# Attention stage: products with reciprocals on another engine, extra work at other steps, fewer and larger transfers, two banks for the last output products

## The reference

```python
q = einsum('bsd,de->bse', layernorm(x), Wq)      # 16 heads of 32
k = einsum('bsd,de->bse', ctx, Wk); v = einsum('bsd,de->bse', ctx, Wv)
qh, kh = rope(split(q)), rope(split(k)); vh = split(v)
attn = softmax(einsum('bhqd,bhkd->bhqk', qh, kh) / sqrt(32))
x = x + einsum('bsd,de->bse', merge(einsum('bhqk,bhkd->bhqd', attn, vh)), Wo)
x = x + ffn(layernorm(x), w_gate, w_up, w_down)  # act_qdq: one scale per whole tensor
```

## Time and profile before

| | us |
|---|---|
| median of 3 runs | 2434.16 (2432.11 to 2439.43) |
| the profiled execution | 2446.6 |
| its span, first to last instruction | 2444.7 |
| PE busy in the span | 2251.5 (92%) |
| DVE / ACT / POOL busy | 1712.5 / 1284.4 / 607.5 |
| attention stage | 0 to 892.5 |

### The profile page before, as it was taken

How to read it: one execution, slowest core, us unless ns; L and a number is a source line. 1 busy time by engine, 2 the same in 40 slices (tenths; PEclk the granted TensorE clock), 3 DMA queues, 4 the chain that set the end, 5 groups by cost and what they waited for, 6 DMA issues and landing times.

```text
span 2444.7 us, 32311 instructions
## 1 busy us (share of the span) xinstructions
PE 2251.5 (92%) x12763; PEld 1002.3 (41%) x12763; DVE 1712.5 (70%) x1750; ACT 1284.4 (53%) x1184; POOL 607.5 (25%) x432
## 2 busy tenths in 40 slices
PE   4698999999998759999999899999999499999999
PEld 2353343333433224444444344444444144444444
DVE  5466788887886646645553179888888797777772
ACT  3235454454543303322332288888887587777771
POOL 2463444444443201100110045444444000000000
PEclk9899999999999979999999999999999799999999
DMA  7443656465555656788876498777778365555551
GB/s 184 108 131 92 169 161 178 142 184 150 163 148 160 152 151 201 243 266 249 269 246 214 176 332 309 291 288 287 289 287 309 147 234 217 216 217 215 217 218 60
DMA packets 307913, 505.57 MB, mean 207 GB/s; under 512 B 208172, under 2 KB 210476, under 8 KB 270892
## 3 DMA queue, kind: packets, MB, share of 16 engines
q1 hardware_dynamic: 307756, 503.45, 62.8%
HBM read 248.83 MB, written 186.65 MB: 178 GB/s over the span
## 4 chain that ended last, share of the span: by engine, by line
PE 78%; DVE 7%; issue 6%; DMA 3%; POOL 3%; ACT 2%; SPq 2%; DVEq 0%; POOLq 0%; ACTq 0%
PE banks L1250 41%; PE banks L1647 19%; PE banks L535 5%; PE banks L577 4%; PE banks L516 2%; PE banks L554 2%; PE banks L594 1%; DVE MX L983 1%; PE banks L599 1%; PE banks L498 1%; DVE A L956 1%; POOL AH L1117 1%; PE banks L495 1%; POOL QW L1076 1%; DMA AH<-in_ctx 1%
## 5 line engine op out<-in xcount | busy, mean ns | idle before, releaser
L1647 PE MATMUL banks<-W,OH 128*128 128x512 f16 x2304 | 501.1, 381 | 37.1 <-DVE OH L1726 37.1
L1250 PE MATMUL banks<-XB,W 128*128 128x512 f16 x2304 | 500.3, 381 | 22.9 <-DMA XB<-XC 22.9
L1250 PE MATMUL banks<-XB,WT 128*128 128x512 f16 x2304 | 500.4, 381 | 8.2 <-DMA XB<-xt_s 8.2
L1270 ACT ACTIVATE OB<-banks,uns 128x512 f32<-128x512 f32 x384 | 254.3, 683 | 425.9 <-PE banks L1250 419.4
L1647 PEld LDWEIGHTS banks<-W,OH 128*128 128x128 f16 x2304 | 226.1, 98 | 312.1 <-issue 39.5
L1250 PEld LDWEIGHTS banks<-XB,W 128*128 128x128 f16 x2304 | 226.1, 98 | 297.1 <-DMA XB<-XC 23.4
L1250 PEld LDWEIGHTS banks<-XB,WT 128*128 128x128 f16 x2304 | 226.1, 98 | 282.5 <-DMA XB<-xt_s 8.7
L1515 POOL TENSOR_TENSOR PR<-GS,OB 128x2048 f32<-128x2048 f32 x47 | 225.4, 4795 | 274.3 <-ACT OB L1270 254.7
L1339 DVE TENSOR_REDUCE amx<-OB 128x1 f32<-128x2048 f32 x48 | 109.7, 2285 | 241.5 <-ACT OB L1270 241.5
L577 PE MATMUL banks<-XC,AH 128*128 128x512 f16 x768 | 182.9, 389 | 16.8 <-DVE RX L943 16.7
L535 PE MATMUL banks<-XD,WQ 128*128 128x512 f16 x768 | 187.2, 396 | 0.0
(11 more groups left out here) (213 smaller groups left out, 2832.8 us busy)
## 6 DMA issues: line engine op xcount, KB each, us to landing
g_s<-OB SPq DMA_DIRECT2D x48, 1024.0 KB, 5.7
GL<-g_s SPq DMA_DIRECT2D x48, 1024.0 KB, 8.2
up_s<-OB SPq DMA_DIRECT2D x48, 1024.0 KB, 4.9
XA<-up_s SPq DMA_DIRECT2D x32, 1024.0 KB, 9.3
gq_s<-GQ SPq DMA_DIRECT2D x48, 512.0 KB, 5.2
XD<-gq_s SPq DMA_DIRECT2D x48, 512.0 KB, 6.7
XA<-in_x SPq DMA_DIRECT2D x16, 1024.0 KB, 7.2
QW<-QE SPq DMA_DIRECT2D x128, 128.0 KB, 2.8
```

Of the source, the lines that this page charges most:

```text
L1250: t = e.matmul(pk[:].rearrange("p (j t) -> p j t", j=4), WT[w][:, ot, wa, kk, :], XB[i % 2][:, xa, :, kk, :], start=(kk == 0 and wa == 0 a ...
L1270: e.activation(OB[n % 3][:, r, :], bank[k % 8][:], ACT.Copy, scale=uns[:, 12 * w + ot:12 * w + ot + 1]).then_inc(s_ev, 1)
L1647: t = e.matmul(pk[:].rearrange("p (r n) -> p r n", r=4), OH[i % 2][:, a, ot, j * 128:(j + 1) * 128], WD[:, :, c, wa, o4, :], start=(ot == ...
```

## The change

- The products of A with the reciprocals (L956) go from DVE to POOL, for all units but the last four. POOL's order in a step becomes: cosine product, products of normal_at(s), sine product, residuals of normal_at(s).
- A unit's reciprocals come by one transfer instead of four.
- In SP's stream X1 is stored before the next x is loaded.
- Weight rows are handled two steps later (w_step(k) = 17 + 4k), so DVE scales in c == 2 steps. A batch's aggregate L970 and the deviation that POOL makes of it go from the c == 3 step to the following c == 0 step, on DVE behind L983 (st2 has two halves).
- The output products of the last eight units run two in a step, in banks 4 and 5 by turns, so there are four steps fewer.
- The last batch's four units are normalised in one step, by DVE, from four buffers of their own (QR); their sums and reciprocals are sent from ACT's queue instead of SP's.
- The weight transposes begin at step 60 instead of 62.

```diff
-NSTEP = NU + 16
+NSTEP = NU + 12
+LATE = NU - 8
...
 def normal_at(s):
     b, c = divmod(s - 13, 4)
-    return [4 * b + 2 * c, 4 * b + 2 * c + 1] if 0 <= b < B and c < 2 else []
+    if s == NSTEP - 4:
+        return list(range(NU - 4, NU))
+    return [4 * b + 2 * c, 4 * b + 2 * c + 1] if 0 <= b < B - 1 and c < 2 else []
+def output_at(s):
+    u = s - 15
+    if u < LATE:
+        return [u] if u >= 0 else []
+    u = LATE + 2 * (u - LATE)
+    return [u, u + 1] if u < NU else []
+def deviations_at(s):
+    if s == NSTEP - 1:
+        return [B - 1]
+    return [output_at(s - 2)[-1] // 4] if output_at(s - 2) and (output_at(s - 2)[-1] + 1) % 4 == 0 and s > 15 else []
 def w_step(k):
-    return 15 + 4 * k
+    return 17 + 4 * k
 def build(nc, x, ctxt, wq, wk, wv, wo, w_gate, w_up, w_down, cosq, sinq, cosk, sink, eye, out, scr):
...
         s_rd = sem("s_rd")
-        s_rb = sems("s_rb", 2)
+        s_rb = sems("s_rb", 4)
...
         rs1 = sbufs(st, "rs1", 2, [128, 8])
-        st2 = sbuf(st, "st2", [128, 4, 6])
+        st2 = sbuf(st, "st2", [128, 2, 4, 6])
...
+        def rb(u):
+            if u < NU - 4:
+                return RB[u % 2][:], s_rb[u % 2], 16 * (u // 2 + 1)
+            i = u - NU + 4
+            return QR[i][:], s_rb[i], 16 * ((NU - 4) // 2 + 1) if i < 2 else 16
+        def o_bank(u):
+            return bank[4] if u >= LATE and u % 2 == 0 else bank[5]
...
-        def sp_recip(e, u):
+        def dma_recip(e, u):
...
             e.wait_ge(s_rd, 16 * (b + 1))
-            if u >= 2:
+            if u >= NU - 4:
+                e.wait_ge(s_c1, NU - 4)
+            elif u >= 2:
                 e.wait_ge(s_an, u - 1)
+            to, sem_, _ = rb(u)
+            e.dma_start(to, sr_d[1 + b % 2, 4 * c:4 * c + 4, :].unsqueeze(1).to_broadcast([4, 32, 512])).then_inc(sem_, 16)
+        def dma_sums_out(e, b):
+            e.wait_ge(s_rc, b + 1)
             for g in range(4):
-                e.dma_start(RB[u % 2][32 * g:32 * g + 32, :], sr_d[1 + b % 2, 4 * c + g:4 * c + g + 1, :].to_broadcast([32, 512])).then_inc(s_rb[u % 2], 16)
+                e.dma_start(sr_d[0, g:16:4, :], RC[32 * g:32 * g + 4, :]).then_inc(s_rg, 16)
+        def dma_sums_in(e, b):
+            e.wait_ge(s_rg, 64 * (b + 1))
+            e.dma_start(RG[:], sr_d[0].rearrange("r (e f) -> (r e) f", f=64)).then_inc(s_rl, 16)
+        def dma_recip_out(e, b):
+            e.wait_ge(s_rr, 2 * (b + 1))
+            e.dma_start(sr_d[1 + b % 2].rearrange("r (e f) -> (r e) f", f=64), RG[:]).then_inc(s_rd, 16)
         def sp_attention(e):
...
-                if c == 3 and 0 <= b - 2 < B:
-                    e.wait_ge(s_rc, b - 1)
-                    for g in range(4):
-                        e.dma_start(sr_d[0, g:16:4, :], RC[32 * g:32 * g + 4, :]).then_inc(s_rg, 16)
+                if c == 3 and 0 <= b - 2 < B - 1:
+                    dma_sums_out(e, b - 2)
                 for u in normal_at(s + 1):
-                    sp_recip(e, u)
-                u = s - 14
-                if 0 <= u < NU:
+                    if u < NU - 4:
+                        dma_recip(e, u)
+                for u in output_at(s - 1):
+                    e.wait_ge(s_x1, u + 1)
+                    e.dma_start(x1_d[u // 4, :, u % 4, :], X1[u % 2]).then_inc(s_x1d[u % 2], 16)
+                for u in output_at(s + 1):
...
                     e.dma_start(XR[u % 2], x1_rows(u // 4)[:, u % 4, :]).then_inc(s_xr[u % 2], 16)
-                u = s - 16
-                if 0 <= u < NU:
-                    e.wait_ge(s_x1, u + 1)
-                    e.dma_start(x1_d[u // 4, :, u % 4, :], X1[u % 2]).then_inc(s_x1d[u % 2], 16)
-                if c == 3 and 0 <= b - 2 < B:
-                    e.wait_ge(s_rg, 64 * (b - 1))
-                    e.dma_start(RG[:], sr_d[0].rearrange("r (e f) -> (r e) f", f=64)).then_inc(s_rl, 16)
+                if c == 3 and 0 <= b - 2 < B - 1:
+                    dma_sums_in(e, b - 2)
...
-                if c == 3 and 0 <= b - 2 < B:
-                    e.wait_ge(s_rr, 2 * (b - 1))
-                    e.dma_start(sr_d[1 + b % 2].rearrange("r (e f) -> (r e) f", f=64), RG[:]).then_inc(s_rd, 16)
+                if c == 3 and 0 <= b - 2 < B - 1:
+                    dma_recip_out(e, b - 2)
...
-                if 62 <= s < 62 + NO:
-                    t = s - 62
+                if 60 <= s < 60 + NO:
+                    t = s - 60
...
         def pe_output(e, u):
             b, j = divmod(u, 4)
-            if u:
+            if u == LATE:
+                e.wait_ge(s_mte, B)
+            elif u > LATE:
+                e.wait_ge(s_x1, u - 1)
+            elif u:
...
                 for wa, a in THREE:
-                    t = e.matmul(BO_, AH[b % 2][:, a, k, j * 128:(j + 1) * 128], WO[:, wa, k, :],
+                    t = e.matmul(o_bank(u), AH[b % 2][:, a, k, j * 128:(j + 1) * 128], WO[:, wa, k, :],
...
                     pe_kv(e, i)
-                if 0 <= s - 15 < NU:
-                    pe_output(e, s - 15)
+                for u in output_at(s):
+                    pe_output(e, u)
...
                     e.activation(RC[:], BS_, ACT.Copy).then_inc(s_rc, 1)
+                    if b - 2 == B - 1:
+                        dma_sums_out(e, B - 1)
+                        dma_sums_in(e, B - 1)
+                        dma_recip_out(e, B - 1)
+                        for u in range(NU - 4, NU):
+                            dma_recip(e, u)
         def dve_amax(e, n):
...
+        def dve_x1_aggregate(e, b):
+            e.wait_ge(s_st2, 12 * b + 10)
+            for i in range(4):
+                t = e.bn_aggr(mv2[:, 4 * b + i, :], st2[:, b % 2, i, :])
+            t.then_inc(s_mv2, 1)
         def dve_v_max(e, g):
...
-                u = s - 16
-                if 0 <= u < NU:
-                    ob, j = divmod(u, 4)
+                for u in output_at(s - 1):
...
                         e.wait_ge(s_st2, 3 * (u - 2) + 3)
-                    e.scalar_tensor_tensor(X1[u % 2], BO_, vun[:, 2:3], XR[u % 2], ALU.mult, ALU.add).then_inc(s_x1, 1)
+                    e.scalar_tensor_tensor(X1[u % 2], o_bank(u), vun[:, 2:3], XR[u % 2], ALU.mult, ALU.add).then_inc(s_x1, 1)
...
                 for u in normal_at(s):
-                    e.wait_ge(s_rb[u % 2], 64 * (u // 2 + 1))
-                    e.wait_ge(s_a, u + 1)
-                    e.tensor_tensor(A[:, u % 6, :], A[:, u % 6, :], RB[u % 2][:], ALU.mult).then_inc(s_an, 1)
-                u = s - 16
-                if 0 <= u < NU:
+                    if u >= NU - 4:
+                        to, sem_, n = rb(u)
+                        e.wait_ge(sem_, n)
+                        e.wait_ge(s_a, u + 1)
+                        e.tensor_tensor(A[:, u % 6, :], A[:, u % 6, :], to, ALU.mult).then_inc(s_an, 1)
+                for u in output_at(s - 1):
...
                     e.wait_ge(s_x1, u + 1)
-                    if j == 0 and ob:
-                        e.wait_ge(s_mv2, ob)
-                    e.bn_stats(st2[:, j, :], X1[u % 2]).then_inc(s_st2, 1)
+                    if j == 0 and ob >= 2:
+                        e.wait_ge(s_mv2, ob - 1)
+                    e.bn_stats(st2[:, ob % 2, j, :], X1[u % 2]).then_inc(s_st2, 1)
...
                     e.tensor_reduce(xmn[:, u:u + 1], X1[u % 2], AX.X, ALU.min).then_inc(s_st2, 1)
-                    if j == 3:
-                        e.wait_ge(s_st2, 3 * u + 1)
-                        for i in range(4):
-                            t = e.bn_aggr(mv2[:, 4 * ob + i, :], st2[:, i, :])
-                        t.then_inc(s_mv2, 1)
+                    if u >= NU - 1:
+                        dve_x1_aggregate(e, ob)
...
+                if s >= 16 and output_at(s - 2) and (output_at(s - 2)[-1] + 1) % 4 == 0 and output_at(s - 2)[-1] < NU - 1:
+                    dve_x1_aggregate(e, output_at(s - 2)[-1] // 4)
...
+                for u in normal_at(s):
+                    if u < NU - 4:
+                        to, sem_, n = rb(u)
+                        e.wait_ge(sem_, n)
+                        e.wait_ge(s_a, u + 1)
+                        e.tensor_tensor(A[:, u % 6, :], A[:, u % 6, :], to, ALU.mult).then_inc(s_an, 1)
+                if s < NU:
+                    pool_rope_sine(e, ROT["q", s])
...
                     e.tensor_tensor(AH[nb % 2][:, 1, nc_, :], A[:, u % 6, :], AH[nb % 2][:, 0, nc_, :], ALU.subtract).then_inc(s_alo, 1)
-                if s < NU:
-                    pool_rope_sine(e, ROT["q", s])
...
                     pool_deviation(e, b + 2)
-                u = s - 19
-                if c == 3 and 0 <= u < NU:
-                    ob = u // 4
+                for ob in deviations_at(s):
...
```

## The result

| | before | after |
|---|---|---|
| median (us) | 2433.14 (2427.72 to 2439.43) | **2560.64** (2558.43 to 2562.72) |
| profiled execution / its span | 2446.6 / 2444.7 | 2561.1 / 2559.3 |
| mean granted clock of TensorE | 0.968 | 0.947 |

The ratio of after to before is 1.0511, 95% interval 1.0495 to 1.0527: 5.1% slower, 127 us by the medians (115 by the two profiled spans, of which the one before was 0.5% over its median). The forecast was 2466 us, range 2438 to 2496. The sign and the new wait were as forecast, the size was not; the time lies 65 us above the range (2560.64 against 2496).

What follows compares the result with a forecast made beforehand. TensorE was taken as the bound, with 47.4 us to win in the attention stretch. +34.8 (stretch) + 5 (first batch) - 8 (tail) = +31.8 us, added to the median 2434.16, gave 2466 us, range 2438 to 2496.

Steps and rivals of the forecast that it cites:

- stretch: Attention from 278.65 to 775.14 us, 46 steps: 12 x (4.85 + 2.0) = 82.2 us in place of 47.4, +34.8 us.
- What bounds the kernel: Attention stretch: TensorE is the bound, 449.1 us without stalls against 496.5, so only 47.4 us can be won.
- The new wait: Each batch: ACT's A copy waits for the first residual, exponential P queues behind, PE stands 4.85 us before the largest-score product.
- landing of the exchange: SP's half exchange QW in the c == 1 step: lands 2.8 us after its second issue, at t = 13.5 from that step's scores.
- rival 3: Exchange leaves right behind QE, both new waits end in time, stall at most 1.4 us: -39 us, 2396 us; chance 0.08.
- rival 4: Products of 1.6 us and landings of 3.9 give a 6.8 us stall and 2.7 us of clock: 2502 us; chance 0.11.
- The issue at t = 11.2: SP, t counted from the c == 1 step's scores: the exchange's second issue was forecast at t = 10.7.
- The clock: TensorE falls to 1.2 GHz after the new wait in all 12 batches, 2.0 us each.
- The tail: Last batch's reciprocals and last eight units' output products: end at about 864.5 us, -8 us, bounds -5 and -12.
- The weights and SP's order: Weight scaling moved to c == 2 on DVE: 0, up to 1 us a batch; SP's store and load order was passed over.
- 1: The stall comes but TensorE's clock holds: +7 us, 2441 us; chance 0.10.
- 2: The copy's wait is covered; ACT's AH and MT, behind GpSimd's products, delay the scores 2.5 us: +1 us, 2435; chance 0.07.

Runs made afterwards that it cites:

- a_resid: Changed kernel with GpSimd's residuals put ahead of the sine product again: 2502.55 us, ratio 1.0294 to the kernel before.
- a_four: Changed kernel with a unit's reciprocals sent by four transfers again instead of one: 2531.99 us, ratio 1.0403 to the kernel before.
- a_two: Changed kernel with a unit's reciprocals sent by two transfers of two source rows each: 2696.67 us, a single run.
- a_dve_order: Changed kernel with four transfers a unit, residuals ahead of the sine product, products on DVE, and SP loading x before storing X1: 2422.03 us, ratio 0.9944.
- a_dve_four: Changed kernel with four transfers a unit, residuals ahead of the sine product and products on DVE: 2441.29 us, ratio 1.0015 to the kernel before.
- a_resid_four: Changed kernel with residuals ahead of the sine product and four transfers a unit: 2476.28 us, ratio 1.0184 to the kernel before.
- b_pool: Kernel before with only the products moved to POOL, residuals staying ahead of the sine product: 2478.36 us, ratio 1.0176.
- b_swap: Kernel before with only SP's order changed, the exchange issued ahead of the reciprocals: 2410.66 us, ratio 0.9889.
- b_weights: Kernel before with only the weight rows handled two steps later: 2421.59 us, ratio 0.9941.
- a_rf_swap: Changed kernel with residuals ahead of the sine product, four transfers a unit and the exchange ahead of the reciprocals: 2448.11 us, ratio 1.0045.
- best: Changed kernel with residuals ahead of the sine product, four transfers a unit, exchange ahead of the reciprocals and products on DVE: 2417.76 us, ratio 0.9919.
- b_swap_pool: Kernel before with the exchange ahead of the reciprocals and products on POOL: 2433.30 us, ratio 0.9985.

## Why the prediction was wrong, step by step

| step | predicted | measured |
|---|---|---|
| product on POOL | 1.30 us | 1.27 |
| exchange's second issue, t | 10.7 | 11.2 (343.31 - 332.08) |
| **its landing** | **2.8, up to 3.9** | **6.5** in this batch, 7.0 mean |
| end of P, t | 18.4 | 22.6 |
| PE's new wait | 4.85 | 9.03 in this batch, 9.4 mean |
| clock behind it | 2.0 | 2.7 |
| stretch | +34.8 | +97.9 |
| ahead of the stretch | +5 | +12.4 |
| tail | -8 | +6.3 |

**What bounds the kernel** held. The free time of the stretch, 449.1 us, fits after too: 594.4 - 449.1 = 145.3, of which 112.4 are waits and 32.9, 2.7 in a batch, are the clock behind them.

**The new wait** was right in its links, though not in the length of one: its place, the queue behind it (the A copy, then P), and that it covers DVE's chain. a_resid, which takes it away, shows that it was the binding one.

**The step that failed is the landing of the exchange**, in the paragraph on SP. It was priced from rows in which the exchange landed 2.81 and 3.92 us after its issue, behind eight transfers of 64 KB, and these were kept when what ran ahead became two of 256 KB. The bytes are the same, but the engines that carry them are not, as a_four and a_two show: four instead of 16. I counted the saved issues (2.7 us of SP's time, and named "for" rival 3) and never asked over how many engines the one transfer would be split, although the diff says it: the source has a leading dimension of four. The error is 3.7 us in this batch's landing. It goes through the chain without a loss: t = 22.6 instead of 18.4 for P's end is 3.7 plus the issue's 0.5. With the clock, 12 x (9.4 + 2.7) - 47.4 = +98 us. The "bounds" were those of one state of the queue, so rival 4 (2502) could not reach the time either.

The number of engines is not all of it. Over the c == 1 steps the landing is 3.6 us in the kernel before, 4.2 in a_four (16 engines, the changed order of SP, products on POOL) and 7.0 in the changed kernel. So of the 4.2 us between 2.8 and 7.0, 2.8 are the four engines, 0.8 come from taking the shorter of two rows (the same step reaches 5.0 us in the kernel before), and 0.6 from what else differs in a_four, most likely SP's order (0.5 us from a_dve_order to a_dve_four). With the transfers on 16 engines the time is still 2531.99 us, above the range, because the later issue (t = 12.8) takes back 1.7 of the 2.8 us.

**The issue at t = 11.2** instead of 10.7: the last reciprocal's issue ended at t = 9.2, as forecast, and from there (341.30) to the exchange's second it is 2.0 us instead of 1.55, since the issues between stand further apart. A large transfer took 0.54 to 0.61 us to issue instead of 0.45; the 1.80 us of the merged row also hold the second one's wait for its product, which ends at 340.65.

**The clock** was mis-sized for its cause: 2.0 us was the mean of eight steps, all after shorter stalls (at most 4.1 us) than these (at least 9.0). The mechanism was right, 12 batches of 12. The Trainium skill's sentence (TensorE: Matmul & The Clock Gate, "HAM oscillation — how this bites in real kernels"), by which a wait that recurs every round costs the clock every round, agrees with these 12.

**The tail** failed in part by the same step. Its four transfers, priced with a landing of 2.8 us, came in one after the other, the products at 955.13, 960.00, 963.00 and 967.07, on four engines. But this is not all. From the copy RC to the last aggregate it is 47.8 us in the changed kernel, in a_resid_four, with 16 transfers, 44.1 (855.70 to 899.78), and before 43.4 (828.84 to 872.28): with the engines back the tail is no longer than before, but the 8 us are not won. There ACT's 16 issues took 8.5 us, and the statistics of earlier units and two aggregates stood on DVE ahead of the last row sums. The prediction counted the row sums from the moment at which the data is there and left out what is already queued on DVE.

**The weights and SP's order** were put at nothing. The first gains 15 us, the second costs 17 to 19 us where the exchange has no slack, and they hid each other.

**The rivals.** 1: no; the clock held in no batch. 2: its path exists and binds in b_pool, at 3.4 to 4.8 us instead of 2.5. 3: an early exchange is indeed worth much (b_swap -26 us, -28 to -34 in the changed kernel), but the change doesn't issue it early, and products on POOL cost 23 to 30 us even with it. 4: right side, too small.

What the parts cost, going down from the changed kernel: the late residual 58.1 us, the one transfer 26.3, products on POOL 35.0 (a_resid_four to a_dve_four), SP's order 19.3; at the other end the weights' shift gains 15.1. That makes 58.1 + 26.3 + 35.0 + 19.3 - 15.1 = 124 us of the 127 measured. The first four terms are steps of one chain down to a_dve_order, so the sum tests only that a_dve_order and b_weights take the same time. The third and fourth are differences between chips; by the ratios they are 41 and 17 us. The order of undoing matters: the transfer costs 43 us on the kernel before, where no other part hides any of it, and the products 41.

**Still open:** by which path products on POOL cost 23 to 30 us when neither the copy nor MX has to wait long for them. For a_rf_swap and best the traces account for it: the stretch is 26.0 us longer (492.8 against 466.7), PE's waits are 36.0 against 16.6 us, which is 19.4, and the other 6.6 follow the waits as lower clock (7.6 us above the free time and the waits, against 1.0). For b_swap_pool and b_swap the two profiled executions are only 7.3 us apart (2426.22 and 2418.89; the medians are 22.6 apart), with the stretch 11.1 us longer (waits 24.6 against 15.6 us), so the traces show only a part of that difference.

One trait separates both pairs in the same way. With products on POOL, ACT's copies AH wait for them (81.7 and 78.3 us of waits in the stretch for A from POOL in b_swap_pool and a_rf_swap, in b_swap and best 5.7 us and none for A from DVE). ACT's two halves of the next x stand behind these copies in its stream, and DVE waits for them in the c == 1 steps: 25.2 and 28.4 us in 11 waits, and not at all in b_swap and best. MX and the row sums come behind that on DVE. This is a path read from waits; no run removes it, so it is not shown as the cause.

## What to carry to other kernels

Before transfers are merged, look at the slowest dimension of both access patterns: a merge that saves issues but leaves four rows outermost puts all bytes on four engines, and in this kernel it was the neighbour in the queue that paid. Price a step that is moved at both ends, what it meets where it arrives and what it frees where it leaves, and check which load or store a reordering puts directly ahead of the transfer on the critical path. When a chain is forecast link by link, put each link's bound from the mechanism, not from the spread of two rows taken under the old conditions.

## What the runs showed of the hardware

- The landing of a transfer of 128 KB behind 512 KB of reciprocals, a store and a load: 4.1 us when the reciprocals were on 16 engines (3.8 to 4.6 over the batches), 6.5 on four (6.5 to 7.3; 98 GB/s plateau), 9.4 on two (8.9 to 9.8; 48 to 55 GB/s plateau).
- A load of 256 KB issued directly ahead of a transfer of the same queue rather than a store delays it by 0.5 us on average (3.65 against 3.18 us), and the load itself lands in 4.3 instead of 3.1 us.
- Issues of the reciprocals from ACT's queue took 0.53 us each for 64 KB (8.5 us for 16) and 0.64 for 256 KB (2.54 for four), against 0.45 and 0.57 (median of 44) from SP's.
- The product with two f32 inputs took 1.27 us on average on POOL (changed kernel) and 0.68 us in the median on DVE (kernel before, 64 of them), there up to 1.77 us, 0.96 on average in the stretch.
